# Moving the zero padding from the scores matmul to the output projection in a transformer layer on eight cores

## What is computed

```python
x = x + attn(layernorm(x))
x = x + ffn(layernorm(x))
# attn: q, k, v = x @ wq.T, x @ wk.T, x @ wv.T; rope over the full width of q and k
scores = einsum('bhqd,bhkd->bhqk', q, k) / math.sqrt(64) + slope[h] * (pos_k - pos_q)
scores = where(causal, -1e9, scores)
out = einsum('bhqk,bhkd->bhqd', softmax(scores), v) ; return out @ out_w.T + out_b
# ffn: block-diagonal 16x16 and 16x64 products for 4 heads x 64 rails, gelu, then h @ w_cproj.T (16384 -> 1024)
```

## Time and profile before

| what | us |
|---|---|
| median of 2 runs | 3258.01 (3243.03 to 3272.99) |
| the profiled execution | 3248.62 |
| span of its slowest core (3) | 3247.1 |
| spans of the eight cores | 3229.6 to 3247.1 |
| TensorE matmul busy | 2155.4 (66%) |
| ScalarE busy | 1055.3 (33%) |
| VectorE busy | 770.2 (24%) |
| GpSimd busy | 236.5 (7%) |

### The profile page before, as it was taken

The page is one execution under the profiler, slowest core; times in us unless marked ns, Lnnn a source line. Parts: engine busy times, 40 slices in busy tenths (PEclk is TensorE's granted clock), DMA queues, the critical chain, the costliest instruction groups (busy, mean ns, idle before and its releaser), DMA issues.

```text
span 3247.1 us, 33637 instructions; the slowest of 8 cores (3229.6 to 3247.1 us)
## 1 busy us (share of the span) xinstructions
PE 2155.4 (66%) x8094; PEld 862.0 (27%) x8094; DVE 770.2 (24%) x1803; ACT 1055.3 (33%) x1967; POOL 236.5 (7%) x449
## 2 busy tenths in 40 slices
PE   0258501733655566666549995697989788898989
PEld 0023200210111112211112221243434344343434
DVE  3310376123444444444422221000000000000000
ACT  1322201102545555555531113532333233332310
POOL 0012100022111111110010000000000000000000
PEclk9999755765556666667765555698999899999999
DMA  1122100036444454442021222588989888898888
GB/s 38 55 32 26 20 0 7 7 57 100 96 92 91 88 97 94 91 92 52 1 39 65 78 69 69 156 266 261 278 265 286 255 260 279 273 282 259 277 288 273
DMA packets 318426, 439.55 MB, mean 135 GB/s; under 512 B 55072, under 2 KB 173856, under 8 KB 318240
## 3 DMA queue, kind: packets, MB, share of 16 engines
q1 hardware_dynamic: 245504, 365.01, 36.2%
q0 software_dynamic: 61216, 47.22, 11.6%
q10 hardware_dynamic: 11520, 25.17, 2.0%
HBM read 425.73 MB, written 58.72 MB: 149 GB/s over the span
## 4 chain that ended last, share of the span: by engine, by line
PE 47%; DVE 16%; DMA 15%; ACT 10%; issue 8%; SPq 2%; DVEq 1%; POOL 1%; ACTq 0%; POOLq 0%
PE pf L1047 19%; DMA wcs<-wcb 12%; PE pat L902 7%; DVE pbuf L731 4%; PE ps L676 4%; PE pqk L380 4%; PE po L753 3%; PE pf L997 3%; ACT ebuf L711 3%; ACT ebuf L718 2%; DMA bbuf<-blkB 2%; PE pc L803 2%; PE pqk L494 2%; DVE rbt L809 1%; SPq L975 1%
## 5 line engine op out<-in xcount | busy, mean ns | idle before, releaser
L1047 PE MATMUL pf<-wcs,Hb 128*128 128x512 bf16 x4096 | 1007.2, 384 | 148.8 <-DMA wcs<-wcb 147.1
L1010 ACT ACTIVATE Hb<-pf 128x256 bf16<-128x256 f32 x1024 | 393.4, 384 | 716.4 <-PE pf L997 691.5
L1047 PEld LDWEIGHTS pf<-wcs,Hb 128*128 128x128 bf16 x4096 | 395.2, 99 | 573.0 <-issue 209.9
L676 PE MATMUL ps<-qstg,KT 128*128 128x512 bf16 x559 | 307.6, 552 | 256.7 <-DVE qstg L668 221.1
L753 PE MATMUL po<-pbuf,Vx 128*65 128x512 bf16 x559 | 308.9, 554 | 98.8 <-DVE Ost L812 80.0
L1064 DVE TENSOR_TENSOR ob<-pf,xr 128x512 f32<-128x512 f32 x32 | 22.1, 692 | 1231.0 <-PE pf L997 876.6
L997 PE MATMUL pf<-btb,w2b 128*128 128x256 bf16 x1024 | 288.1, 288 | 37.5 <-issue 15.6
L902 PE MATMUL pat<-owt,Ost 64*128 64x512 bf16 x512 | 224.1, 629 | 22.6 <-DMA owt<-owT 22.6
L718 ACT ACTIVATE ebuf<-ps,cpool 128x512 bf16<-128x512 f32 x303 | 208.2, 687 | 87.2 <-PE ps L676 56.5
L711 ACT ACTIVATE ebuf<-ps,cpool 128x1024 bf16<-128x1024 f32 x128 | 142.7, 1115 | 281.9 <-PE ps L676 262.3
L676 PEld LDWEIGHTS ps<-qstg,KT 128*128 128x128 bf16 x559 | 70.7, 127 | 451.9 <-issue 443.2
(11 more groups left out here) (99 smaller groups left out, 1250.1 us busy)
## 6 DMA issues: line engine op xcount, KB each, us to landing
wcs<-wcb SPq DMA_DIRECT2D x1024, 256.0 KB, 4.9
wcv<-wcT POOLq DMA_DIRECT2D x256, 128.0 KB, 3.1
wcb<-wcv SPq DMA_DIRECT2D x256, 128.0 KB, 1.7
w2b<-w2scr SPq DMA_DIRECT2D x256, 128.0 KB, 3.6
xin<-x SPq DMA_DIRECT2D x16, 512.0 KB, 4.4
xrb<-x SPq DMA_DIRECT2D x16, 512.0 KB, 5.6
xres<-xnw ACTq DMA_DIRECT2D x16, 512.0 KB, 5.8
xr<-xres SPq DMA_DIRECT2D x16, 512.0 KB, 6.8
```

The source lines that it names most:

```text
L676: P.op("tensor", (lambda p_=pr, f_=hf, kc_=kc, hc_=hc, qp_=qc % 2: (lambda e: e.matmul(ps[p_][:, 512 * f_:512 * (f_ + 1)], KT[0:128, S * h ...
L1010: P.op("scalar", (lambda m_=mc, z_=zb, p_=p: (lambda e: e.activation(Hb2[p_][:, SB2 * m_:SB2 * (m_ + 1)], pf[z_][:, 0:SB2], AF.Gelu, bias= ...
L1047: P.op("tensor", (lambda m_=mc, s_=sl2, e_=e2, pi=pb_i, i_=i, p_=p: (lambda e: e.matmul(pf[pi][:], Hb2[p_][:, SB2 * m_ + 128 * s_:SB2 * m_ ...
```

## The change

The staging of the queries goes away: the scores matmul reads the 64 partitions of the head from KT and QT directly. The output projection gets 128 rows: Ost and owt become 128 partitions high, partitions 64 to 127 are zeroed once by VectorE, and its matmuls take all 128. The row of sums is now copied into sqd (float32 instead of bf16, also the discarded output of the layer norm's squares), from which the Ln reads; its copy no longer waits for the broadcast of the job before. rbt becomes float32.

```diff
-    sqd = es.enter_context(nc.sbuf_tensor("sqd", [128, 1024], BF16))
+    sqd = es.enter_context(nc.sbuf_tensor("sqd", [128, 1024], F32))
...
-    Ost = p3_es.enter_context(nc.sbuf_tensor("Ost", [64, NH * S], BF16, side="right"))
+    Ost = p3_es.enter_context(nc.sbuf_tensor("Ost", [128, NH * S], BF16, side="right"))
...
-    qstg = [p3_es.enter_context(nc.sbuf_tensor(f"qstg{i}", [128, 512], BF16, side="right"))
-            for i in range(2)]
...
-    rbt = [p3_es.enter_context(nc.sbuf_tensor(f"rbt{i}", [128, 512], BF16, side="right"))
+    rbt = [p3_es.enter_context(nc.sbuf_tensor(f"rbt{i}", [128, 512], F32, side="right"))
...
-        if first:
-            qp = qc % 2
-            P.op("vector", (lambda p_=qp, hb_=hb: (lambda e: e.memset(
-                qstg[p_][64 - hb_:128 - hb_, :], 0.0)))(),
-                 waits=[qs_free[qp]], inc="v")
-            P.op("vector", (lambda p_=qp, hb_=hb, hc_=hc, qc_=qc: (lambda e: e.tensor_copy(
-                qstg[p_][hb_:hb_ + 64, :],
-                QT[hb_:hb_ + 64, S * hc_ + 512 * qc_:S * hc_ + 512 * (qc_ + 1)])))(),
-                 waits=[rope_evt[("q", hc)]], inc="v")
-            qs_evt[ji] = P.now("v")
...
-            KT[0:128, S * hc_ + 128 * kc_:S * hc_ + 128 * (kc_ + 1)],
-            qstg[qp_][:], start=True, stop=True)))(),
-             waits=[rope_evt[("k", hc)], qs_evt[ji],
+            KT[hb_:hb_ + 64, S * hc_ + 128 * kc_:S * hc_ + 128 * (kc_ + 1)],
+            QT[hb_:hb_ + 64, S * hc_ + 512 * qc_:S * hc_ + 512 * (qc_ + 1)],
+            start=True, stop=True)))(),
+             waits=[rope_evt[("q", hc)], rope_evt[("k", hc)],
                     ps_free[pr] if hf == 0 else None], inc="t")
...
-    P.op("vector", lambda e: e.memset(rrow[64:66, :], 1.0), inc="v")
+    P.op("vector", lambda e: e.memset(sqd[64:66, :], 1.0), inc="v")
     ev_sq65 = P.now("v")
+    P.op("vector", lambda e: e.memset(Ost[64:128, :], 0.0), inc="v")
+    ev_ost0 = P.now("v")
...
-                rrow[64:65, 512 * p_:512 * (p_ + 1)], po[p_][64:65, :])))(),
-                 waits=[ev_av, ev_vconst, drow_evt[pob], rrow_evt[pob]], inc="v")
+                sqd[64:65, 512 * p_:512 * (p_ + 1)], po[p_][64:65, :])))(),
+                 waits=[ev_av, ev_vconst, drow_evt[pob]], inc="v")
...
-            rrow[64:66, 512 * p_:512 * (p_ + 1)],
+            sqd[64:66, 512 * p_:512 * (p_ + 1)],
             AF.Ln, bias=0.0, scale=1.0)))(),
...
-    owt = p3b_es.enter_context(nc.sbuf_tensor("owt", [64, NH * 1024], BF16, side="right"))
+    owt = p3b_es.enter_context(nc.sbuf_tensor("owt", [128, NH * 1024], BF16, side="right"))
...
+    P.op("vector", lambda e: e.memset(owt[64:128, :], 0.0), inc="v")
+    ev_owt0 = P.now("v")
...
-                    Ost[0:64, S * h_ + 128 * s_:S * h_ + 128 * (s_ + 1)],
-                    owt[0:64, 1024 * h_ + 512 * e_:1024 * h_ + 512 * (e_ + 1)],
+                    Ost[0:128, S * h_ + 128 * s_:S * h_ + 128 * (s_ + 1)],
+                    owt[0:128, 1024 * h_ + 512 * e_:1024 * h_ + 512 * (e_ + 1)],
```

More of the change, by code:

```diff
@@ L606, in build_nc @@
     pb_free = [None] * 4
-    qs_free = [None, None]
-    qs_evt = {}
     pend_s = []
@@ L675, in stage1 @@
         chunk_slot[cj] = (pr, hf, pair_no[0] % 4)
-        P.op("tensor", (lambda p_=pr, f_=hf, kc_=kc, hc_=hc, qp_=qc % 2: (lambda e: e.matmul(
+        P.op("tensor", (lambda p_=pr, f_=hf, kc_=kc, hb_=hb, hc_=hc, qc_=qc: (lambda e: e.matmul(
             ps[p_][:, 512 * f_:512 * (f_ + 1)],
-            KT[0:128, S * hc_ + 128 * kc_:S * hc_ + 128 * (kc_ + 1)],
-            qstg[qp_][:], start=True, stop=True)))(),
-             waits=[rope_evt[("k", hc)], qs_evt[ji],
+            KT[hb_:hb_ + 64, S * hc_ + 128 * kc_:S * hc_ + 128 * (kc_ + 1)],
+            QT[hb_:hb_ + 64, S * hc_ + 512 * qc_:S * hc_ + 512 * (qc_ + 1)],
+            start=True, stop=True)))(),
+             waits=[rope_evt[("q", hc)], rope_evt[("k", hc)],
                     ps_free[pr] if hf == 0 else None], inc="t")
         pend_s.append((cj, P.now("t")))
-        if last:
-            qs_free[qc % 2] = P.now("t")
         if hf == 1 or last:
@@ L899, in build_nc @@
             pi = (sl % 2) * 2 + e2
-            wts = [ev_owt, ev_browb, pat_free[pi]] + [ost_evt[(h, qcsl)] for h in range(NH)]
+            wts = [ev_owt, ev_owt0, ev_ost0, ev_browb, pat_free[pi]] + [ost_evt[(h, qcsl)] for h in range(NH)]
             for h in range(NH):
```

## The result

The changed kernel takes 3090.72 us (median of 11 runs, 3072.85 to 3196.72) against 3254.49 us before (median of 10). The ratio is 0.9476 with a 95% interval of 0.9446 to 0.9506: 5.2% faster. Three of the 11 executions, 3119.57 to 3196.72, were slower because the cores of one die ran at a lower clock, and the ratio leaves such ones out. Run again on another occasion it came out at 0.9491 (0.9442 to 0.9541). The forecast was 3110 us, range 3020 to 3200.

The account below looks back on a forecast made before the run. Attention was taken to be held by TensorE's waits for qstg and Ost, the output projection by its 0.50 clock. From 3248.6, -57 + 19 - 100 gave 3110.6, left at 3110 us, range 3020 to 3200.

Parts of the forecast that it names:

- Part 1: Attention: scores without staging remove the qstg waits; matmuls 0.55 us apart at clock 0.50, 825 us against 882, 57 less.
- the decay tiles: Attention: ScalarE computes five once a head in 3.4 us, about 1.3 of it shows, 20 us in all.
- the last pairs: End of attention: they have nothing beside them, 5 us.
- Part 2: Ahead of attention: zeroing Ost takes 27.4 us on VectorE, so the first values matmul starts 19 us later.
- Part 3: Output projection over 128 rows: the clock rises, a slice takes 11.5 us instead of 17.94, 100 us less.
- just fits: Output projection: layer norm of the slice before takes 7.4 us, and the transposes needing it come after 7.8.
- Part 4: The rest: zeroing owt, 13.7 us, hides behind its load; types, squares, Ln and row copy cost about nothing.
- The empty pipe: Rival in attention: going between 64 and 128 rows costs more, 0.76 a matmul, 234 us slower, 3345; chance 0.05.
- Zeros don't count: Rival in the output projection: the clock goes by nonzero work and stays at 0.50, 3211 us; chance 0.12.
- The clock stays up in attention: Rival: attention keeps 0.66, matmuls at some 0.45 instead of 0.55, 3030 us; chance 0.07.
- No price for a change of rows: Rival in attention: a change of rows costs nothing, 133 us less, some 35 given back, 3012 us; chance 0.06.

Follow-up runs that it names:

- e12_zero_32bit: Changed kernel with both zeroings, still on VectorE, written as float32, half as many elements for the same bytes; 3071.13 us, ratio 0.9402.
- e9_heads_paired: `e8_staged_ahead` with two heads side by side in Ost and owt, 8 real 128-row matmuls instead of 16, nothing zeroed; ratio 0.9297.
- e4_scores128_unstaged: Changed kernel with scores over all 128 partitions, without staging, so the output differs; 3060.5 us, attention 693 to 699 us.
- e8_staged_ahead: Kernel before with queries staged one job ahead, 128-row output projection and Ost zeroed by GpSimd; ratio 0.9315.
- e5_values64: Changed kernel with the values matmul over only 64 of its 128 rows, half the sum left out; attention 700 us.
- e10_rows_grouped: Changed kernel with Ost zeroed by GpSimd and two values matmuls, then two scores matmuls, where they alternated; ratio 0.9361.

## Why the prediction was right

**Part 1, attention.** The mechanism and the price of TensorE's stream held: waits for qstg gone, the clock at 0.50 from end to end, spacings 0.54 and 0.56 where 0.55 was used. The stream was forecast at 740 us, and TensorE's busy time is 740.6. Forecast for the stage 825, measured 793. The difference is in the waits, which I had summed from nearby stalls, 85 us where 52 came: for Ost 60, measured 44.2; for the decay tiles 20, where all waits for exponentials in attention come to 4.4; for the last pairs 5, measured 2.5. That ScalarE's 3.4 us of tiles hardly show is, as I read it, because TensorE goes on meanwhile with the other ps buffer; no run tests this. So the term was -57 and turned out -88, and attention ended near 1605 and not 1634.

**Part 2, the zeroing.** Forecast +19, measured +25. The time by the row was exact (27.4 forecast, 27.36 shown), but the row does not hold the whole: 34.3 us pass. I had taken 0.834 ns an element from the durations of two short memsets. The distance between neighbouring instructions would have been the better source. The Trainium skill, "VectorE: DVE Perf Modes", Zero memsets can be issued as uint32 (trn2), says a memset takes one cycle per element whatever the type; at the 0.96 GHz that the page gives for VectorE that is an estimate of 34.1 us. It agrees with the 34.3, and the section's advice to write zeros as 32-bit words agrees with the 17.25 of `e12_zero_32bit`. I had not used that rule.

**Part 3, the output projection.** Forecast -100, measured -110. The zero rows raise the clock (0.94). A slice took 11.0 on the mean where I had put 11.5; 0.7 was my allowance, mostly for the clock falling in the transposes, and with 0.94 over the stage and most slices at 10.4 to 10.9 it fell seldom. The estimate of 0.32 for a change of rows at the full clock stands: the bias matmul starts 3.54 after the first of sixteen, which is 15 x 0.216 + 0.30, and the next follows 0.32 later. The remark that the layer norm "just fits" holds: in `e9_heads_paired`, with half the matmuls, TensorE waits for it in every slice.

**Part 4.** The zeroing of owt hides behind its load (21.6 us of wait, 22.6 before). The types cost nothing to be seen: the Ost product shows 0.68 us as before. No run takes them and the row copy apart from the scores, but two things speak against a share in the 88 us: before the change no idle time ahead of the row copy (L763) ended with a broadcast, 22.3 us of it with a values or scores matmul; and the wait for Ost is 107 us in `e4_scores128_unstaged` with them and 118 in `e8_staged_ahead` without.

**The sum.** -57 + 19 - 100 = -138 against -88 + 25 - 110 = -173 by stages and -164 between the medians. All three terms have the right sign, and together they are 35 us too small. That the time is only 19 us below the forecast is in part luck: the feed-forward part and the way to the output projection came out 9 us longer for other reasons, and the kernel before is at 3254.5 in ten runs where I had started from 3248.6.

**The rivals.** The empty pipe (0.76 a matmul) is refuted by the 0.54 and 0.56. Zeros don't count: refuted by 0.94. The clock stays up in attention: refuted by 0.50. The clock doesn't need the changes of rows to stay low: `e5_values64`, a stream of 64-row matmuls nearly without them, has 0.50 too, and so has `e10_rows_grouped` with half of them. No price for a change of rows: refuted by the spacings, and by the 58 us that `e10_rows_grouped` takes out of the stream. By the Trainium skill, "TensorE: Matmul & The Clock Gate", Why this matters for your kernels, a continuously busy TensorE gets the full clock; at 93% busy attention did not get it, and the measurement decides.

Still open: how much of the 93 us in `e5_values64` is the change of rows and how much the overlap in odd heads. And whether two heads' scores could be put side by side on purpose, as the overlap suggests, was not tried.

## What to carry to other kernels

At the same clock a 512-column matmul took 0.43 us with 64 rows and with 128, but in this kernel the rows helped to decide the clock: padding the output projection with zero rows took 110 us out of 295 and added no matmul. The opposite holds beside it: taking zero rows out of the scores lost the share of full clock there (0.66 before, 0.73 in `e4_scores128_unstaged`, 0.50 now), and paid only because it also removed a stall at each job's start. Before removing padding, ask what clock the stretch has and whether its neighbours have the same rows; before removing a stall, add up TensorE's own stream at the lower clock, since that is what is left.

A large memset's cost is read from end to end of its neighbours, and not from its row.

## What the runs showed of the hardware that I had not expected

- A memset on VectorE shows four fifths of its time as busy: 27.36 of 34.3 us for 32768 elements, 13.71 of 17.25 for 16384. The rest is idle time before it, put down to ScalarE or to no one.
- The clock of the output projection rose with the rows: 0.50, 0.78 and 0.94 with 64, 96 and 128 rows, the same work and zeros in what was added. It also fell with the share of time that TensorE was busy: 0.78 with 128 rows and half the matmuls, at 69% busy instead of 85%.
- Two 64-row matmuls that take different halves of the partitions start within 0.03 us of each other; with the same half they stand 0.43 apart, with 64 and 128 rows 0.55.
